# Cross-attention and block-quantised FFN on one core: transposes by DMA, another order on POOL, and a shorter quantisation of the hidden rows

## The reference

```python
def block_quant(v, m_bits, bk):
    vb = v.reshape(*lead, K // bk, bk)
    amax = max(abs(vb), axis=-1, keepdims=True)
    e = floor(log2(maximum(amax, 2.0 ** -126)))
    scale = exp2(e - m_bits)
    return (round(vb / scale) * scale).reshape(v.shape)

def lowprec_linear(x, w, b, m_bits, bk):
    return einsum('bsk,nk->bsn', block_quant(x), block_quant(w)) + b

x = x + xattn(layernorm(x), ctx)           # 16 heads, causal mask, projections with biases
h = gelu(lowprec_linear(layernorm(x), w_fc, b_fc, 3, 32))
x = x + lowprec_linear(h, w_proj, b_proj, 3, 32)
```

## Time and profile before

| | us |
|---|---|
| median of three runs | 258.28 |
| lowest and highest | 257.05, 261.14 |
| the profiled execution's own time | 255.91 |
| its span on the core | 254.1 |
| PE busy | 215.5 (85%) |
| DVE busy | 209.6 (82%) |
| ACT busy | 180.6 (71%) |
| POOL busy | 119.3 (47%) |

### The profile page before, as it was taken

One profiled execution on the slowest core, in us unless ns is written; L12 is line 12 of the kernel. 1 busy time (PEld: TensorE's weight loads), 2 busy tenths in 40 slices (PEclk: granted clock), 3 DMA queues, 4 the chain that ended last, 5 costly groups with the idle time before them and its releaser, 6 DMA issues.

```text
span 254.1 us, 6527 instructions
## 1 busy us (share of the span) xinstructions
PE 215.5 (85%) x2128; PEld 162.1 (64%) x2136; DVE 209.6 (82%) x880; ACT 180.6 (71%) x462; POOL 119.3 (47%) x120
## 2 busy tenths in 40 slices
PE   7895798979985999599999999979759599489974
PEld 7784666758763776477687787757327357356743
DVE  4444599997799599769989989899998995999981
ACT  2336888878965687668798898899746456668972
POOL 2700014535049506920370371362636395479893
PEclk9999999997999799889999999999989859999999
DMA  6682663842343044214414324323013001001112
GB/s 203 152 275 62 203 158 83 238 91 55 94 94 76 18 93 89 71 28 88 78 49 99 66 50 98 71 38 60 3 18 70 23 22 41 23 21 41 44 41 83
DMA packets 38001, 20.39 MB, mean 80 GB/s; under 512 B 13125, under 2 KB 37713, under 8 KB 37969
## 3 DMA queue, kind: packets, MB, share of 16 engines
q1 hardware_dynamic: 34896, 17.17, 28.7%
q10 hardware_dynamic: 3072, 2.82, 3.5%
HBM read 7.61 MB, written 2.11 MB: 38 GB/s over the span
## 4 chain that ended last, share of the span: by engine, by line
PE 36%; DVE 25%; issue 12%; SPq 10%; POOL 7%; DMA 5%; ACT 3%; ACTq 1%; POOLq 0%; DVEq 0%
PE bank L1010 8%; DVE prob L777 7%; POOL hq L678 4%; PE bank L1117 4%; PE s_banks L1059 4%; DVE probT L786 4%; PE s_banks L1075 3%; SPq L251 3%; PE bank L1098 3%; DMA w_rows<-in_L_xattn_Wq 2%; PE bank L986 2%; PE s_banks L1225 2%; SPq L258 2%; DVE hrn L952 2%; PE bank L1075 2%
## 5 line engine op out<-in xcount | busy, mean ns | idle before, releaser
L429 ACT ACTIVATE prob<-prob,negm 128x128 f32<-128x128 f32 x256 | 80.8, 391 | 19.4 <-DVE negm L777 19.2
L777 DVE CUSTOM_DVE_ANT_0 prob<-s_banks,mask_f 128x128 f32<-128x128 f32 x256 | 58.7, 285 | 14.0 <-PE s_banks L1059 13.9
L678 POOL TENSOR_TENSOR hq<-hrn,h_mag 128x1024 bf16<-128x1024 f32 (+1 forms) x17 | 31.2, 1836 | 20.5 <-DVE hrn L952 20.2
L1010 PE MATMUL bank<-cT,wT 128*128 128x256 f32 x128 | 33.2, 406 | 0.0
L1059 PE MATMUL s_banks<-KS,QC 16*128 16x128 f32 x512 | 23.3, 295 | 11.6 <-issue 5.5
L1059 PEld LDWEIGHTS s_banks<-KS,QC 16*128 16x128 f32 x512 | 17.3, 185 | 20.8 <-issue 20.8
L514 ACT ACTIVATE s_banks<-s_banks 128x512 f32<-128x512 f32 x32 | 17.9, 580 | 14.5 <-PE s_banks L1225 14.1
L1010 PEld LDWEIGHTS bank<-cT,wT 128*128 128x128 f32 x128 | 25.6, 210 | 3.2
L573 POOL TENSOR_TENSOR XQ<-xr,x_mag 128x512 bf16<-128x512 f32 x8 | 8.4, 1048 | 38.6 <-DVE xr L850 38.6
L786 DVE COPY probT<-s_banks 128x512 f32<-128x512 f32 x31 | 21.3, 686 | 3.2 <-PE s_banks L1075 3.2
L564 POOL TENSOR_TENSOR rs<-ve,neg_half 128x2 f32<-128x2 f32 x8 | 5.6, 698 | 38.8 <-DVE ve L726 38.4
(11 more groups left out here) (124 smaller groups left out, 447.1 us busy)
## 6 DMA issues: line engine op xcount, KB each, us to landing
oden<-oT SPq DMA_DIRECT2D x60, 64.0 KB, 2.4
KS<-full SPq DMA_DIRECT2D x32, 64.0 KB
VS<-full SPq DMA_DIRECT2D x64, 32.0 KB, 2.0
out<-full SPq DMA_DIRECT2D x16, 128.0 KB, 1.7
QS<-full SPq DMA_DIRECT2D x29, 64.0 KB, 2.3
X<-in_x ACTq DMA_DIRECT2D x1, 1536.0 KB, 7.6
cbuf<-in_ctx SPq DMA_DIRECT2D x6, 256.0 KB, 4.4
fc_rows<-in_L_ffn_w_fc SPq DMA_DIRECT2D x1, 1024.0 KB, 6.2
```

The costliest lines, as they stand in the source:

```text
L429: ins = nc.scalar.activation(prob[:, k % 4, u, s, :], prob[:, k % 4, u, s, :], ACT.Exp, bias=negm[:, k % 4, u, s:s + 1], scale=-1.0)
L678: nc.gpsimd.tensor_tensor(blocks(hq[par][:, some]), blocks(hrn[par][:, some]), spread(h_mag[par][:, n * nb:(n + 1) * nb], nb), ALU.subtract)\
L777: V.tensor_tensor_reduce(prob[:, k % 4, u, s, :], s_banks[:, 2 * (k % 2) + u, s * P:(s + 1) * P], mask_f[:, :], 1.0, LARGEST, ALU.add, ALU ...
L1010: ins = T.matmul(proj_bank(p, t)[:, c * PT:(c + 1) * PT], wT[:, t, k, c, :], src[:, k, :], start=(k == 0), stop=(k == KC - 1))
```

## The change

Six parts:

1. The transposes of the weights and of the quantised rows leave PE and ACT. SP issues DMA transposes from SBUF to SBUF: two of 128x1024 bf16 (256 KB) for each weight matrix, and one of 128x512 bf16 (128 KB) for each pair's rows (`transpose_rows`). The first matrix and pair 0 stand at the head of step 7 in SP's stream, ahead of `move_out(6)`; the second matrix and pairs 1 to 4 behind it; pairs 5, 6 and 7 at the head of tiles 0, 3 and 9. `trans_weights`, `copy_weights`, `trans_q` and `copy_tq` are gone. `ffn_up(0)` waits for all four weight transposes, and every second `ffn_up` for its pair's rows.
2. POOL rounds the weight parts 3 to 5 and 6 to 7 ahead of `round_rows` and `power1` of their steps.
3. In the FFN, DVE takes the block maxima in two halves, each as soon as its half of gelu is done, into PSUM; one instruction (`half_up`) masks the exponent and sets the next lower bit, which makes 1.5 times the power of two; the additions multiply by 2^20 themselves (`scalar_tensor_tensor`). The magic number that POOL subtracts is computed by ACT (`magic`, an activation of 128x32), behind gelu(t+1) in ACT's order.
4. On DVE the residual and statistics of pair 7 go behind the additions of tile 6, the quantisations of pairs 6 and 7 behind the additions of tiles 3 and 8 (`round_rows(7)` on POOL to tile 9). The normalised rows of pairs 6 and 7 lie in PSUM.
5. The last two sequences add their residual in place in X and no longer wait for an earlier store.
6. The last sequence's half transposes go to two other PSUM banks.

The core of the diff:

```diff
-        xqT = [sb(f"xqT{n}", [P, KC, P], bf16) for n in range(2)]
+        xqT = sb("xqT", [P, B, KC, P], bf16)
...
+        def half_up(eng, dst, src):
+            return eng.tensor_scalar(dst.bitcast(i32), src.bitcast(i32), 0x7F800000, 0x00400000, ALU.bitwise_and,
+                                     ALU.bitwise_or)
...
+        ROWS_AT = {0: NPAIR - 3, 3: NPAIR - 2, 9: NPAIR - 1}
...
+            def transpose_rows(p):
+                sp.wait_ge(sm["xq_done"], p + 1)
+                sp.dma_start_transpose(xqT[:, 2 * p:2 * p + 2, :, :].rearrange("p b k t -> p (b k) t"),
+                                       XQ[:, 2 * p:2 * p + 2, :].rearrange("p b e -> p (b e)"))\
+                  .then_inc(sm[f"xqt{p}"], 16)
+            def transpose_fc():
+                sp.wait_ge(sm["fc_ready"], 4)
+                for n in range(2):
+                    sp.dma_start_transpose(wfcT[:, 4 * n:4 * n + 4, :, :].rearrange("p a k m -> p (a k) m"),
+                                           fc_q[:, 4 * n:4 * n + 4, :].rearrange("p a e -> p (a e)"))\
+                      .then_inc(sm["wt_in"], 16)
+            def transpose_pj():
+                sp.wait_ge(sm["fc_ready"], 8)
+                for f in range(2):
+                    sp.dma_start_transpose(wpjT[:, :, f * P:(f + 1) * P], pj_q[:, f, :]).then_inc(sm["wt_in"], 16)
             def step(i, par, first, last):
+                if last:
+                    transpose_fc()
+                    transpose_rows(0)
...
+                if last:
+                    transpose_pj()
+                    for p in range(1, NPAIR - 3):
+                        transpose_rows(p)
...
             def tile(t, par, first, last):
+                if t in ROWS_AT:
+                    transpose_rows(ROWS_AT[t])
...
                 if not last:
                     gelu(t + 1, 1 - par)
-                if t < B - 2:
-                    copy_tq(t + 2, par)
+                magic(t, par)
...
+            def magic(t, par):
+                act.wait_ge(sm["h_exp_done"], t + 1)
+                if t >= 2:
+                    act.wait_ge(sm["hq_done"], t - 1)
+                nc.scalar.activation(h_mag[par][:, :], h_exp[par][:, :], ACT.Copy, scale=RAISE)\
+                    .then_inc(sm["h_mag_done"], 1)
...
-                if i == 1:
-                    for u in range(3):
+                if 1 <= i < 4:
+                    for u in range(3 * i - 3, min(3 * i, 8)):
                         round_weights(u)
                 if i > 2:
                     round_rows(i - 3)
                 if ahead(i):
                     power1(i + 2)
-                if i == 2:
-                    for u in range(3, 6):
-                        round_weights(u)
-                if i == 3:
-                    for u in range(6, 8):
-                        round_weights(u)
...
                     pool.wait_ge(sm["h_round"], 2 * t + 2 if not last else 2 * t + 1 + n)
+                    pool.wait_ge(sm["h_mag_done"], t + 1)
...
+                for n in range(2):
+                    dve.wait_ge(sm["gelu_done"], 2 * t + n + 1)
+                    V.tensor_reduce(h_amax[:, 16 * n:16 * n + 16], blocks(bank[2 * par + n][:, :]), axis=AX.X,
+                                    op=ALU.max, apply_absolute_value=True).then_inc(sm["h_amax_done"], 1)
+                dve.wait_ge(sm["h_amax_done"], 2 * t + 2)
                 if t >= 2:
-                    dve.wait_ge(sm["hq_done"], t - 1)
-                quant_mag(V, h_mag[par][:, :], exps).then_inc(sm["h_mag_done"], 1)
+                    dve.wait_ge(sm["h_mag_done"], t - 1)
+                half_up(V, h_exp[par][:, :], h_amax).then_inc(sm["h_exp_done"], 1)
...
                 for n in range(2):
-                    V.tensor_tensor(blocks(hrn[par][:, 512 * n:512 * n + 512]), blocks(bank[2 * par + n][:, :]),
-                                    spread(h_mag[par][:, 512 // BLK * n:512 // BLK * (n + 1)], 512 // BLK), ALU.add)\
+                    V.scalar_tensor_tensor(blocks(hrn[par][:, 512 * n:512 * n + 512]),
+                                           spread(h_exp[par][:, 512 // BLK * n:512 // BLK * (n + 1)], 512 // BLK),
+                                           RAISE, blocks(bank[2 * par + n][:, :]), ALU.mult, ALU.add)\
                         .then_inc(sm["h_round"], 1)
                 if t == 2:
                     stats2(NPAIR - 2)
+                if t in (3, LAST_OUT + 3):
+                    quantise(NPAIR - 2 + t // LAST_OUT)
+                    quantise_rest(NPAIR - 2 + t // LAST_OUT)
                 if t == LAST_OUT - 1:
                     normalise_last()
+                if t == LAST_OUT + 1:
+                    residual(NPAIR - 1)
+                    stats2(NPAIR - 1)
...
             def ffn_up(t, par):
-                pe.wait_ge(sm["tq_copied"], t + 1)
+                if t % 2 == 0:
+                    pe.wait_ge(sm[f"xqt{t // 2}"], 16)
+                if t == 0:
+                    pe.wait_ge(sm["wt_in"], 64)
```

More of the change, by code:

```diff
@@ L74, in build_program @@
         pj_q = sb("pj_q", [P, KC, HID], bf16)
-        wfcT = sb("wfcT", [P, KC, HID], bf16)
+        wfcT = sb("wfcT", [P, HID // P, KC, P], bf16)
         wpjT = sb("wpjT", [P, HID // P, E], bf16)
@@ L1164, in step @@
                 transpose_probs(k + 1)
-                if last:
-                    trans_weights(2)
-                else:
+                if not last:
                     project(i + 1, 1)
```

141 lines of the change are left out of this document (31 added, 110 removed).

## The result

The changed kernel takes 249.53 us (median of four runs, 248.59 to 250.06); the kernel before took 259.69 us beside it. Timed once more on another chip it was 248.9 against 258.25, ratio 0.963 [0.956, 0.970]. The forecast of 246.5 us is 0.954 of the 258.28 that it stood against: right in sign and within its range, about 1% too low.

The account below looks back on a forecast made before the run. Bounds: DVE in step 7 and the FFN; POOL's late `queries_apart` and PE's lower clock in steps 2 to 4. Terms -7.0, -0.5, +1.6, -2.4, -2.3, -0.2 sum to -10.8 from 255.9, plus 1.4: 246.5 us; range 239 to 257.

Parts of the forecast that it names:

- rival (c): FFN gives nothing, or POOL's order only its waits; 4 to 6 us missing, 250.5 to 252.5 us; chance 0.20.
- (d): The forecast itself: whole kernel at 240 to 250 us; chance 0.62.
- Part 1: Steps 2 to 4: POOL rounds weights ahead of `power1`; -2.0, -3.3 and -1.7, sum -7.0 us.
- The price: Steps 2 and 3: DVE work slowed beside POOL's moved rounding; 0.9 us added to each.
- Part 2: Step 7: weights and first rows leave PE and ACT; at most 1.25 us (DVE's idle time), -0.5 taken.
- Part 3: Step 7 to FFN: DMA transposes delay `ffn_up(0)` by 4.5 h - 7.8 us; +1.6 taken.
- h: Time one 256 KB DMA transpose holds SP's queue; 2.1 us taken, bounds 0.64 and 5.11.
- (a): Transposes slow on SP's queue: h 8.5 or 17.1 us, kernel 274 or 312 us; chance 0.08.
- (b): Transposes cost what eight value moves cost: h near 4 to 5.1 us, kernel 254 to 259; chance 0.10.
- the 1.4 us that the forecast adds: Whole kernel: added to 245.1 us because the profiled execution lay below the three runs, giving 246.5.
- Part 4: DVE's tile in the FFN: magic number goes, maxima halved; -0.19 us a tile, thirteen tiles count, -2.4 us.
- Part 5: FFN, last pairs' norms: the 2.48 us wait for `project_out(7)` goes; net -2.3 us, between -1 and -4.

Follow-up runs that it names:

- e1: Kernel before with POOL's new order of weight rounding alone; ratio 0.983 [0.971, 0.994] to the kernel before.
- h0: Changed kernel timed again, unchanged, on another chip; 248.9 us against 258.25 for the kernel before, ratio 0.963 [0.956, 0.970].
- e2: Changed kernel with the FFN's maxima, magic number, additions and last pairs' norms as before; ratio 0.982 [0.973, 0.992] to the kernel before.
- e4: Changed kernel with 30 idle products on PE ahead of `ffn_up(2)`; ratio 0.965 [0.951, 0.979] to the kernel before.

## Why the prediction was right, and where it was not

The time fell inside the range, and its total is in part luck. By the two profiles 4.8 of the forecast's 10.8 us are missing, as much as rival (c) expected (4 to 6), and 249.53 us lies 0.5 below the upper end of (d). Most of what is missing went the way of that rival: the FFN gave little.

**Part 1** was right in its mechanism: both waits are gone, and e1 shows steps 3 and 4 of the changed kernel with nothing else changed. That -7.2 was measured for -7.0 is chance: the same three steps are 8.7 us shorter in h0 and 5.4 in e1, with step 2 at a clock of 1.00 and 0.85. The price was mis-sized by step: 0.9 was put on each; step 2 pays 0.3 (19.21 against 18.88 at a clock of 1.00), step 3 pays 2.0, with a norm in it that stretched by 1.6 to 2.35 us. In the profile of e1 2.6 us of the gain are lost again in step 7, which the forecast did not see; it is one execution.

**Part 2** failed in its bound. DVE's 1.25 us of idle time was taken as what is left in step 7; the step ends 8.6 us behind lden, over POOL's `power2(5)`, and DVE was only nearly full beside that. Of ACT's and PE's freed work nothing came out.

**Part 3**: h was 1.36 us, below the 2.1 taken, so by the prediction's own sum (4.5 h - 7.8) `ffn_up(0)` waits for nothing, and it did not. Its packets were as taken: 8,576 more on the queue for 2.1 MB, some 245 bytes each; 64 of them for each of 16 DMA engines in 1.36 us make 21 ns a packet, where the queue's 33 had been taken. What failed is the place where the queue's delay was counted: `move_out(6)` stands behind 2.5 transposes, and its own landing releases ACT's inversion, on which the step hangs. It cost 1.1 there (8.01 less 6.92). The longer issues cost 0.64 more, which no run ties to the change; together with landing that is +1.86. So the forecast of +1.6 came nearly true by luck, by a route that was not in it. Rivals (a) and (b) fell with h (their times leave out the 1.4 us that the forecast adds). By the 1309 ns for one 128x128 block in the Trainium skill's "VectorE: DVE Perf Modes", section "The three transpose paths", eight blocks would have held the queue 10.5 us, by an estimate; the trace has 1.36 us, and the data landed 3.3 to 4.1 us after the issue. The Trainium skill's "Advanced Engine Details and Errata", section "X-Bar Transpose (TRN2)", is the nearer one, though 256 KB in 1.36 us are 193 GB/s, about half of its 350 to 400.

**Part 4**: the tile was right, 2.76 us where 2.91 - 0.19 = 2.72 was forecast. The count was not. Tiles 0, 1 and 9 to 15 gave 1.2 us in all (3.78 to 3.65, 3.16 to 3.02, six tiles 17.45 to 16.71, and 0.15 in the last); tiles 5 to 8 hold another 0.6, tiles 2 to 4 none. The tail gave 0.7 back: PE's lower level behind tile 8's quantisation, carried to the end by engines that need 2.74 us of a tile of 2.75; in h0, where the clock held, nothing was given back. That was rival (c) in part: POOL's tile is full, and the delay reached it over `magic`.

**Part 5** came out in size, but not by its own working: tiles 5 to 8 fell from 20.0 to 16.9 us, of which 0.6 are the shorter tile, so -2.5 against -2.3. Yet in e2, which leaves the norms where they were, these tiles take 18.3 us: 1.8 went without this part, since DVE stood 0.71 instead of 2.48 us for `project_out(7)` there. So against e2 this part is worth some 0.8 us. The step that failed is the one that took the 2.48 us as a wait that goes for nothing: its length is not fixed, since DVE and PE come to it at other times (1.02 us in e1). Missing altogether was PE's clock at `project_out(6)`, +1.6 in tile 2. e4 shows that work on PE ahead of it can hold the clock; e1, which has all of PE's transposes, lost 0.7 us there as well, so that the missing transposes are the cause is not shown.

Together the FFN: -1.2 - 2.5 - 0.6 (the shorter tiles 5 to 8) + 1.6 (tile 2) + 0.1 (tiles 3 and 4) + 0.7 (tail) = -1.9 from rounded terms, -1.8 by the span.

## What to carry to other kernels

Before pricing a transfer added to a queue, list what stands behind it on that queue and follow each to the engine that waits, not only the transfer's own reader. In a step that hangs on a round trip (queue, ACT, POOL, queue), busy time of any engine says nothing; look for an interval that stays constant, here 8.6 us from lden to the FFN, and then for the instruction in it that stands late only by its place in a stream. A wait may be what is left of another engine's lateness: before counting it as a gain, ask what else moves it. And where PE stands idle ahead of a product that others wait for, ask what that product takes at the lower clock level.
